# A two-layer graph network on one core: picked rows start one and two chunks earlier, and unread products stand before TensorE's late waits

## What is computed

```python
x = _layernorm(x + L0(x, edge_attr_3, W, root, gamma, beta, edge_index))
x = _layernorm(x + L1(x, edge_attr_64, src, dst, W1, b1, W2, b2, bn_gamma, bn_beta))
# L0: spline convolution, the mean over incoming edges, batch norm, ELU
weights, idx = _spline_basis(edge_attr)             # 8 weights for each edge
B = zeros((E, 8)).at[arange(E)[:, None], idx].add(weights)
z = (B[:, :, None] * x[src][:, None, :]).reshape(E, 8 * 64)
agg = segment_sum(z @ W.reshape(8 * 64, 64), dst)
out = agg / maximum(cnt, 1)[:, None] + x @ root     # then batch norm and ELU
# L1: the sum over incoming edges of node + edge features, then an MLP
agg = segment_sum(node_feats[src] + edge_feats, dst)
h = relu(agg @ W1 + b1) @ W2 + b2                   # then batch norm
```

## Time and profile before

| | |
|---|---|
| median of 3 executions | 568.96 us (564.38 to 569.73) |
| the profiled execution, its span | 569.5 us, 567.5 us |
| TensorE products busy | 514.2 us (91%) |
| VectorE busy | 461.0 us (81%) |
| ScalarE busy | 365.4 us (64%) |
| GpSimd busy | 345.8 us (61%), 354 gathers |
| mean granted TensorE clock | 0.945 |

### The profile page before, as it was taken

How to read it: one execution, slowest core, us unless ns; L and a number is a source line. 1 busy time by engine, 2 the same in 40 slices (tenths; PEclk the granted TensorE clock), 3 DMA queues, 4 the chain that set the end, 5 groups by cost and what they waited for, 6 DMA issues and landing times.

```text
span 567.5 us, 14904 instructions
## 1 busy us (share of the span) xinstructions
PE 514.2 (91%) x4651; PEld 421.6 (74%) x4651; DVE 461.0 (81%) x1745; ACT 365.4 (64%) x662; POOL 345.8 (61%) x362
## 2 busy tenths in 40 slices
PE   5287989899999999999999999999998896999992
PEld 2175878788888888889888888888877775444532
DVE  7989788889888888977888988888878844879865
ACT  8557767687777788767787877878544232620144
POOL 6777777777777777777777777777777700000000
PEclk9998889999999999999999999999999555899998
DMA  7543445455555555555554655654362100000002
GB/s 152 122 98 76 121 106 141 112 133 139 137 133 138 139 128 136 141 130 139 127 137 125 152 126 134 151 126 134 68 122 57 28 6 2 0 2 0 2 1 56
DMA packets 91424, 56.41 MB, mean 99 GB/s; under 512 B 76250, under 2 KB 77685, under 8 KB 91347
## 3 DMA queue, kind: packets, MB, share of 16 engines
q1 hardware_dynamic: 78829, 43.59, 30.1%
q0 software_dynamic: 11328, 11.62, 10.8%
q10 hardware_dynamic: 1190, 0.23, 0.2%
HBM read 54.41 MB, written 1.00 MB: 98 GB/s over the span
## 4 chain that ended last, share of the span: by engine, by line
PE 73%; DVE 11%; ACT 7%; issue 3%; DMA 3%; DVEq 2%; ACTq 1%
PE ps L667 14%; PE ps L721 14%; PE ps L626 12%; PE ps L677 7%; PE ps L651 7%; PE ps L897 6%; PE ps L645 2%; PE ps L902 2%; DVEq L1342 2%; DMA codes_scratch<-z_room 2%; DVE agg L1347 1%; PE ps L634 1%; DVE pair L1332 1%; ACT whot_room L1002 1%; PE ps L656 1%
## 5 line engine op out<-in xcount | busy, mean ns | idle before, releaser
L555 POOL DMA_INDIRECT rows<-in_x,idx x354 | 344.6, 973 | 109.0 <-issue 96.6
L721 PE MATMUL ps<-whot_room,rows 128*128 128x96 f32 x816 | 165.3, 286 | 1.9 <-issue 1.7
L1028 ACT ACTIVATE u<-u,own 128x768 uint8<-128x768 uint8 (+1 forms) x168 | 153.3, 968 | 21.1 <-DMA u<-codes_scratch 21.1
L626 PE MATMUL ps<-pair,ohp 128*125 128x300 bf16 (+1 forms) x416 | 141.0, 342 | 20.7 <-DVE ohp L1336 12.4
L1043 ACT CAST adj<-ps 125x500 f32 x208 | 124.0, 596 | 42.1 <-PE ps L634 25.6
L721 PEld LDWEIGHTS ps<-whot_room,rows 128*128 128x128 f32 x816 | 131.2, 200 | 6.6 <-issue 2.2
L1332 DVE TENSOR_SCALAR pair<-iota_h,comb 128x300 bf16<-128x300 int16 (+1 forms) x416 | 104.1, 312 | 10.4 <-PE ps L634 7.0
L1336 DVE TENSOR_SCALAR ohp<-iota_h,srcp 128x125 bf16<-128x125 int16 x416 | 110.0, 280 | 0.6 <-issue 0.4
L667 PE MATMUL ps<-xs,u 125*128 125x192 bf16 x1050 | 107.0, 248 | 0.0
L667 PEld LDWEIGHTS ps<-xs,u 125*128 125x128 fp8e4 x1050 | 87.8, 99 | 4.0
L1347 DVE TENSOR_TENSOR agg<-agg,ps 128x24 f32 x416 | 75.3, 181 | 14.9 <-PE ps L651 6.1
(11 more groups left out here) (213 smaller groups left out, 452.4 us busy)
## 6 DMA issues: line engine op xcount, KB each, us to landing
u<-codes_scratch SPq DMA_DIRECT2D x42, 400.0 KB, 4.1
rows<-in_edge_attr SPq DMA_DIRECT2D x51, 256.0 KB
more_codes<-codes_scratch SPq DMA_DIRECT2D x20, 400.0 KB
rows<-in_x,idx POOLq DMA_INDIRECT x354
x_now<-in_x SPq DMA_DIRECT2D x25, 31.2 KB
adj<-in_x SPq DMA_DIRECT2D x1, 700.0 KB
xs<-in_x SPq DMA_DIRECT2D x1, 700.0 KB
out<-u SPq DMA_DIRECT2D x3, 224.0 KB
```

The costliest lines, as they stand in the source:

```text
L555: pool.indirect_dma_start(rows[:, s, t, 0:C], None, x, bass.IndirectOffsetOnAxis(ap=idx[:, at:at + 1], axis=0)).then_inc(gathered[0][0] if ...
L626: return nc.tensor.matmul(m_ps[0:PN, bank_of(g), 0:PAIRS].rearrange("p (j w) -> p j w", w=GWIN)[:, :, low:low + WIDTHS[n]], ohp[:, par, t, ...
L721: last = nc.tensor.matmul(z_ps[:, half, at:at + ZW], rows[:, s, t, :], whot[:, par, t, :], start=True, stop=True)
L1028: last = nc.scalar.activation(of, of, ACT.Abs_reciprocal_sqrt, bias=own[:, 0:1], scale=SHARP)
```

## The change

The first kind of pick begins with chunk 4 (TAKE_FROM 5 to 4), the second with chunk 6 (MORE_FROM 8 to 6; it follows TAKE_FROM, with + 2 in place of + 3). The picked rows become 43 and 21 (42 and 20 before), and GpSimd's gathers 352 (354). `keep_busy` makes products of ident with iota_h, 500 columns each, into a bank of z_ps that is free. Four stand at tile 0, at tile 4 and at the end of each of chunks 46 to 50, four at each of two waits of `last_chunk`, two before the wait for `h_summed` and eight before that for `relu_added`: 78 in all.

```diff
-    TAKE_FROM, TAKE_TO = SLOTS + 1, NCH - SLOTS - 1
+    TAKE_FROM, TAKE_TO = SLOTS, NCH - SLOTS - 1
+    BUSY_FROM, BUSY = TAKE_TO - 1, 4
-    MORE_FROM = TAKE_FROM + 3
+    MORE_FROM = TAKE_FROM + 2
...
+            def keep_busy(bank, n):
+                for _ in range(n):
+                    nc.tensor.matmul(ps[:, bank, 0:PAIRS], upper_halves(ident[:, :]), iota_h[:, 0:PAIRS].bitcast(BF16),
+                                     start=True, stop=True)
...
                     if t % (CH // 2) == 0:
+                        pe.wait_ge(zsb_ready, c * 2 + (half + 1))
+                        if c >= BUSY_FROM:
+                            keep_busy(half, BUSY)
                         pe.wait_ge(gathered[s][half], second_half(c, s) if half else i * GATHERED + GATHERED)
-                        pe.wait_ge(zsb_ready, c * 2 + (half + 1))
...
+                if c >= BUSY_FROM:
+                    pe.wait_ge(zsb_ready, c * 2 + 3)
+                    keep_busy(0, BUSY)
                 pe.wait_ge(added, c * CH + CH)
...
                 half = slice(0, half_of)
+                keep_busy(0, BUSY)
                 pe.wait_ge(gathered[s][0], i * GATHERED + GATHERED)
...
                     if n == 0:
+                        keep_busy(1, BUSY)
                         pe.wait_ge(gathered[0][0], (i + 1) * GATHERED + STEP * 16)
...
             begin_squares()
+            keep_busy(1, BUSY // 2)
             pe.wait_ge(h_summed, 1)
...
+            keep_busy(1, WARM - STEP * STEP)
             pe.wait_ge(relu_added, 1)
             for _ in range(WARM):
                 unread(7)
```

## The result

The changed kernel takes **577.37 us**, the median of 6 executions (575.17 to 580.24). The kernel before, run beside it on the same chip, takes 568.07 us (563.95 to 573.0). The ratio is 1.0181, with a 95% interval of 1.0138 to 1.0224: slower, though the interval leaves open whether by 2%. Each ratio in this document is taken over the executions in the faster of the chip's two states and each median over all of them, so a ratio need not be the quotient of two medians. The profiled execution took 577.84 us, its span is 576.0 us, its mean granted clock 0.966 for 0.945. So the clock is higher over the whole and the time is longer all the same.

A forecast was written before the change was run, and what follows sets the result against it. TensorE was taken to pace the picked chunks and, at half clock, 442 to 470 us. Span 567.5 + 10.2 (shift) - 1.6 (after 441.59) - 1.5 (tail) = 574.6, + 2.0 around it = 576.5 us; range 564 to 585.

The forecast's parts named there:

- ScalarE +3.1 and the wait for the table: Chunks 2 and 3: ScalarE's copy of pairs ends 3.1 us later, and chunk 3, waiting for the table, begins 7.9 us later.
- The shift: From chunk 7 on, TensorE runs +10.2 us late (8.0 to 12.4) through stall and picks, and does not make it good.
- GpSimd would then be held by its slots: Mid-program: GpSimd, about a chunk ahead, would wait for slots and end about where it does now.
- Fillers, and after 441.59: Chunks 46 to the last: fillers push TensorE 5.7 us late but keep the clock; the stretch after 441.59 nets -1.6 us.
- the turn of the sums: After 441.59, before chunk 50: a step of 4.56 us that at full clock would take 2.5 us.
- The tail: Last stage: full clock on the chain would give 2.1 us, with possible loss in the late products; -1.5 us (-2.1 to +1.5).
- GpSimd paces after all: Rival, whole kernel: GpSimd sets the pace, so two gathers fewer pay and fillers are hidden; 558 us, chance 0.12.
- idle room on it gives nothing: From 105 to 411 us: GpSimd's rows come 7 us before TensorE's products, so two gathers fewer, 2.5 us, are worth nothing.
- Absorbed: Rival, chunks 4 to 12: shrinking waits absorb the early stall and only the 50 picks cost, some 3 us; 569.5 us, chance 0.22.
- The clock falls anyway: Rival, as the last chunk begins: it takes 17.6 us in place of 10.7 and the tail gives nothing; 585 us, chance 0.12.

The follow-up runs named there:

- e4: The changed kernel with the three parts of the table made one chunk earlier, fillers kept; 569.91 us, ratio 1.0094 to the kernel before.
- e1: The changed kernel without any of the 78 unread filler products, so the earlier picks alone; 576.99 us, ratio 1.0173 to the kernel before.
- e6: The kernel before with the second kind of pick begun at chunk 12 in place of 8, no fillers; 567.45 us, ratio 1.0024.
- e10: The kernel before with second picks from chunk 12 and SyncE's late loads issued once the last chunk's products are done; 571.47 us, ratio 1.007.
- e2: The kernel before with the 78 unread filler products added, picks from chunks 5 and 8 as before; 567.79 us, ratio 0.9992.
- e5: The kernel before, unchanged, run and profiled once more; 567.92 us, ratio 1.0002.
- e9: The changed kernel without the two groups of fillers in the tail, all other fillers kept; 575.62 us, ratio 1.0148 to the kernel before.
- e12: The kernel before with SyncE's late loads alone moved, to once the last chunk's products are done; 568.52 us, ratio 1.0001.
- e7: The kernel before with fillers only in chunks 49, 50 and the last one, none in the tail; 564.58 us, ratio 0.9988.

## Why the prediction was right, and where its terms were off

Forecast 576.5 us, measured 577.4; the profiled 577.84 us against a sum of 576.5. Step by step:

**ScalarE +3.1 and the wait for the table.** Right in mechanism and nearly in size. The copy that was to end at 49.9 us ended at 48.31 + 0.58 = 48.9, 2.1 later than before and not 3.1, since ScalarE's part of the table ahead of it began at 43.70 for 44.73 in this execution; from there on it is 3.2 later. VectorE's half began at 50.30 for 47.68, +2.6. `xs` was to be ready at 56.4 and was at 55.96; chunk 3 was to begin at 56.5 and began at 56.02. The standstill "nearly 5" was 4.64 us. e4 takes both stands away, and 6.5 us of chunk 46's delay go with them.

**The shift.** Predicted +10.2 (8.0 to 12.4), the profile has +8.6 at chunk 7 (93.98 for 85.39), +8.9 at chunk 44 (404.21 for 395.36), 8.7 at chunk 46, and over all kernels it is 424.5 - 414.8 = 9.7 there. By first products: the start of chunk 3 +7.5 for +7.9, then chunk 3 +0.1 for +0.9, chunk 4 +2.4 for +1.8, chunk 5 +0.1 for +0.2, chunk 6 -1.6 for -0.6. It was not made good on the way.

**"GpSimd would then be held by its slots": wrong.** Chunk 44's last gather ended at 389.00 us and its products began at 404.21, 15 us after it where it had been 7, and POOL still shows issue alone ahead of it. It had that much room in its slots. In e1, with the same picks, a slot does hold it a few times, for 1.02 us at most:

```profile
124.02 0.94 POOL L556 DMA_INDIRECT rows<-in_x,idx  x1 [1.02 <-PE ps L729]
```

This changed no term of the sum.

**Fillers, and after 441.59.** The standstills of 4.6 us did go, the clock was kept. From chunk 46 to chunk 50 the delay grew by 2.1 us, by my steps 3.6 (5.7 late, and the turn of the sums 2.1 shorter). From chunk 50, its four first fillers included, to the count it took 18.8 us for 24.2, -5.4, where my steps make it -5.2. So this term was -3.4 and I said -1.6; against the mean of the profiles without fillers it is -1.0, so the -3.4 is partly the luck of the profile that I started from. One reading was wrong: of the two stands "before" the fall only the first was. The 1.55 us that end at 441.59 begin at 440.04, and the clock fell at 440.0.

**The tail.** Predicted -1.5 (-2.1 to +1.5); it was +3.0, outside. From the count to the products nothing came of the 2.1 us, since the clock fell at 475.6 us, just as the count began: 1.83, 1.87 and 1.25 us again. Then the 175 products lost 3.0, twice what I had allowed. Against the profile the errors are -1.5 (the shift at chunk 46), -1.8 and +4.5: the sum is better than its parts, and that it lies within 1.3 us of the profile is luck. By the means over the profiles the change is +9.7 and -1.0, with 0 to 3.0 us in the 175 products, for the 9.3 us between the medians.

**The rivals.** *GpSimd paces after all* (0.12): not in the changed kernel, where from chunk 3 on a chunk's fourth gather ends 14 to 20 us before the chunk's first product. But my reason against it was read at chunk 44 alone, and "idle room on it gives nothing" is too strong. By the same measure the kernel before has 3.8 us at chunk 6, 9.8 at chunk 44 and 2.5 at chunk 49, where the last gather is down to the 1.5 us of a landing. In the middle the two go almost equally fast: two chunks are 13 gathers, 306 / 241 x 13 = 16.5 us on GpSimd, and (395.36 - 93.94) / 18 = 16.7 us on TensorE (first products of chunks 8 and 44; the former is 0.17 us behind its head in the earlier trace rows), so the distance hardly changes there. e6 spends it: its chunk 44 begins at 391.33, before that chunk's last gather has ended (390.87 + 0.99 = 391.86).

```profile
391.33 0.36 PE L721 MATMUL ps<-whot_room,rows 128*128 128x96 f32 x2
```

```profile
390.87 0.99 POOL L555 DMA_INDIRECT rows<-in_x,idx  x1 [0.30 <-issue]
```

So the delay of the changed kernel, ahead of chunk 47, is paid in full, while a gain there can at most use up that distance. A forecast of a gain from these rows would have been wrong, as those of e6 and e10 were, each with a second cause beside this one (the collision; the low clock). *Absorbed* (0.22): against it stand e1, 1.0173, and the shift kept over 40 chunks. *The clock falls anyway* (0.12): it held until 475.6 us, past the last chunk.

**What the clock costs.** By the Trainium skill (TensorE: Matmul & The Clock Gate, "What's actually happening") activity releases the throttle. That the clock is held by work fits chunks 46 to 50: without standstills no fall (the row of 423 to 452 us), in e2 as in the changed kernel. The release does not show as simply here: e5's clock stayed low with TensorE busy for all of 13.3 us, and e9, with less work ahead of the 175 products, met them at 1.0 where the changed kernel met them at 0.5.

## What to carry to other kernels

When work starts earlier, look first at what it needs that is built once: here a table that was ready 3.7 us before its use (53.33 for 57.01) became a wait of 4.6, and through three engines its order cost 6.5 us, twice the 3.2 that are left with the early table. Before speeding up the engine that paces, read how far ahead its supplier is at every stage, the first and the last too; the smallest distance, not the usual one, caps the gain. And a stretch of low clock in one profile isn't a price: profile the unchanged kernel twice before paying for fillers to remove it.

## What the runs showed of the hardware

- The clock stayed at 0.5 from 438.1 to 489.3 us in e10, with TensorE busy for 44.6 of 51 us; in e5, the kernel before once more, it was 13.6, then 20.5 us, with 10 us of full clock between, and in the kernel before 47.8 us on end. The fall comes at nearly the same place (438.7 to 440.0 us in before, e5, e12), its length doesn't repeat.
- Rows of a gather, normally there 1.5 us after its instruction, took 5.6 us in e6 while two loads of 781 KB in all, issued on SyncE's queue, were under way, and 4.2 us in e10 behind loads of 687 KB.
- Executions of one and the same program up to chunk 46 (before, e2, e5, e7, e12) reach it at times that differ by 2.2 us, though from 105 to 411 us TensorE has products in work for 302.75 to 304.25 us in each of them.
